# Layer norms joined with the stages behind them, and router products turned round, in a four-layer GNN and feed-forward kernel

## The reference

```python
def _layernorm(x, axis=-1, eps=1e-05):
    m = jnp.mean(x, axis=axis, keepdims=True)
    v = jnp.var(x, axis=axis, keepdims=True)
    return (x - m) / jnp.sqrt(v + eps)

x = x + _L0_gnn_ref(_layernorm(x), ...)   # edge softmax over 4 heads
x = x + _L0_ffn_ref(_layernorm(x), ...)   # the 1561 rows with the highest x @ wr + br pass a gelu MLP (256, 1024, 256)
x = x + _L1_gnn_ref(_layernorm(x), ...)   # attention with edge features, q, k, v and skip products
x = x + _L1_ffn_ref(_layernorm(x), ...)   # 32 experts, each row goes to the argmax of its logits
x = x + _L2_gnn_ref(_layernorm(x), ...)   # filter convolution, batch norm
x = x + _L2_ffn_ref(_layernorm(x), ...)   # 8 dense experts of three layers, mixed by a softmax
x = x + _L3_gnn_ref(_layernorm(x), ...)   # graph attention, batch norm
x = x + _L3_ffn_ref(_layernorm(x), ...)   # shared MLP and 4 experts, the two best gated
```

## Time and profile before

| | |
|---|---|
| median of 3 runs | 4507.1 us (4505.77 to 4510.82) |
| profiled execution | 4520.46 us, its span 4518.6 us |
| busy: PE, DVE, ACT, POOL | 3633.8, 2836.9, 1719.1, 2510.1 us |
| PE's weight loads (beside PE) | 2915.3 us |
| granted PE clock, mean | 0.861 |
| DMA | 790.42 MB, mean 175 GB/s |

### The profile page before, as it was taken

One profiled execution on the slowest core, in us unless ns is written; L12 is line 12 of the kernel. 1 busy time (PEld: TensorE's weight loads), 2 busy tenths in 40 slices (PEclk: granted clock), 3 DMA queues, 4 the chain that ended last, 5 costly groups with the idle time before them and its releaser, 6 DMA issues. The chain is left out here.

```text
span 4518.6 us, 75485 instructions
## 1 busy us (share of the span) xinstructions
PE 3633.8 (80%) x20890; PEld 2915.3 (65%) x20890; DVE 2836.9 (63%) x6154; ACT 1719.1 (38%) x3863; POOL 2510.1 (56%) x2542
## 2 busy tenths in 40 slices
PE   5997579879999999527399999479999677877288
PEld 4765457667878878425288888367777466666165
DVE  8877566458898898741488888343333345554753
ACT  3765422203333333212266666233333223333132
POOL 6885767667777777464577776200000277776300
PEclk8755779989999999758699999779999778888589
DMA  9565256279999999535488887220000167776400
GB/s 210 187 214 178 82 157 200 71 251 323 336 335 335 332 335 335 176 91 157 123 237 244 239 242 222 88 66 0 0 0 0 59 183 212 208 212 202 113 15 28
DMA packets 661732, 790.42 MB, mean 175 GB/s; under 512 B 151811, under 2 KB 584051, under 8 KB 657812
## 3 DMA queue, kind: packets, MB, share of 16 engines
q1 hardware_dynamic: 369553, 300.43, 22.6%
q0 software_dynamic: 117920, 308.04, 22.5%
q10 hardware_dynamic: 174083, 179.76, 12.9%
HBM read 516.89 MB, written 275.42 MB: 175 GB/s over the span
## 5 line engine op out<-in xcount | busy, mean ns | idle before, releaser
L2831 POOL DMA_INDIRECT fl_far<-x_table,fl_index x416 | 459.6, 1105 | 150.8 <-issue 126.5
L1596 POOL DMA_INDIRECT by_dst<-dst_row,place x416 | 434.9, 1045 | 182.8 <-issue 103.7
L2219 POOL DMA_INDIRECT a_far<-kv_table,a_index x416 | 440.3, 1058 | 140.8 <-issue 124.5
L2554 POOL DMA_INDIRECT a_far<-src_table,a_index x416 | 416.5, 1001 | 131.7 <-issue 123.1
L2868 PE MATMUL ps<-fl_w,fl_hid 128*128 128x256 f32 x1664 | 399.6, 383 | 25.7 <-ACT ps L2940 24.9
L3664 POOL DMA_INDIRECT starts<-p_out,p_at x25 | 24.7, 986 | 705.1 <-DMA starts<-p_zero 697.4
L2253 PE MATMUL ps<-a_w,a_edge_t 128*128 128x256 f32 x1664 | 397.2, 382 | 0.0
L2868 PEld LDWEIGHTS ps<-fl_w,fl_hid 128*128 128x128 f32 x1664 | 310.3, 191 | 70.7 <-issue 31.2
L2253 PEld LDWEIGHTS ps<-a_w,a_edge_t 128*128 128x128 f32 x1664 | 302.7, 192 | 33.1
L1223 ACT ACTIVATE f_hid<-ps,f_bn 128x320 f32<-128x320 f32 x320 | 197.6, 617 | 327.3 <-PE ps L1177 327.3
L1264 DVE SCALAR_TENSOR_TENSOR x_sb<-ps,f_cw,x_sb 128x256 f32 x200 | 96.8, 484 | 342.7 <-PE ps L1188 342.7
(11 more groups left out here) (583 smaller groups left out, 9314.3 us busy)
## 6 DMA issues: line engine op xcount, KB each, us to landing
partial<-a_out ACTq DMA_DIRECT2D x208, 546.0 KB
a_edge<-by_dst SPq DMA_DIRECT2D x104, 516.0 KB
partial_f<-fl_out ACTq DMA_DIRECT2D x26, 2056.0 KB
dst_row<-in_edge_attr SPq DMA_DIRECT2D x52, 1024.0 KB
xn_sb<-q_table SPq DMA_DIRECT2D x416, 128.0 KB
fl_keys<-key_rows SPq DMA_DIRECT2D x26, 1024.0 KB
a_keys<-local_rows SPq DMA_DIRECT2D x104, 128.0 KB
m_far<-kv_table SPq DMA_DIRECT2D x15, 640.0 KB, 7.2
```

Of the source, the lines that this page charges most:

```text
L1596: self.nc.gpsimd.indirect_dma_start(out=self.table, out_offset=bass.IndirectOffsetOnAxis(ap=self.place[:, n:n + 1], axis=0), in_=self.row[ ...
L2219: gathered[b % 4].count(nc.gpsimd.indirect_dma_start(out=far[:, b, u, :], out_offset=None, in_=kv_table, in_offset=bass.IndirectOffsetOnAx ...
L2554: gathered[b].count(nc.gpsimd.indirect_dma_start(out=far[:, b, u, :], out_offset=None, in_=src_table, in_offset=bass.IndirectOffsetOnAxis( ...
L2831: gathered[q * 4 + t // 4].count(nc.gpsimd.indirect_dma_start(out=far[:, q, t, :], out_offset=None, in_=table, in_offset=bass.IndirectOffs ...
```

## The change

1. `norm_stage` becomes a class `Norm` with a program part for each engine; only n4 is still a stage. The parts of n1, n2, n3, n5, n6 and n7 stand at the head of f0, p1, f1, f2, p3 and f3, so six stages end less. PE turns pair i and then follows with the products of the tiles of pair i - 2, once their copies are there. The norm has 4 (f0, f1), 6 (f2, f3) or 2 banks (p1, p3). In p1 and p3 ACT norms all tiles and copies all pairs.
2. `Router` (f1, f2, f3): 512 turned tokens (a quad of tiles) are the moving operand and the router's weights, with zeros at both sides, the stationary one, so that several quads add up in one bank, each in its own lines. ACT (in f1 also DVE) copies the lines to SBUF, PE turns them back, DVE adds the bias. The zeros are laid by POOL.
3. f0: wr, broadcast to 128 columns, is the stationary operand; each quad's product is the key row itself in all partitions. DVE adds the bias into `key_row` between its copies; PE turns 25 pieces of one line into columns for `wgt`. DVE waits for wr and br before the norm.
4. Router weights have a semaphore of their own; PE waits for the others behind the routing. f2 loads `bo` last.
5. p3's preparation (score weights, indices, zeroing of `starts` in 8 parts from a memset of 416 columns) moves to f2: SP's loads behind f2's, DVE's operations between the softmax weights and the loop. p3's copies are all DVE's, its products have 6 banks.
6. p1 has 6 banks that rotate.
7. Shares: place 27, f0 20, p1 6, f1 10 with AHEAD = 5.

```diff
+    def tensor(self, pe, follow):          # class Norm
+        BEHIND = 2
+        for i in range(self.PAIRS + BEHIND):
+            if i < self.PAIRS:
+                self.wait_normed(pe, self.tiles_of(i)[-1] + 1)
+                if i >= self.banks:
+                    self.wait_copied(pe, i - self.banks)
+                for a in self.tiles_of(i):
+                    for k in range(KD):
+                        at = (2 * k + a % 2) * P
+                        last = self.nc.tensor.transpose(self.ps[:, self.first_bank + i % self.banks, at:at + P], self.xn[:, a, k * P:(k + 1) * P], self.ident)
+                last.then_inc(self.transposed, 1)
+            if i >= BEHIND:
+                self.wait_copied(pe, i - BEHIND)
+                for a in self.tiles_of(i - BEHIND):
+                    follow(a)
...
+        if self.by_act == TILES:            # Norm.scalar, behind the last root
+            take_pairs(2, 5)
+            norm(11, 19)
+            take_pairs(5, 9)
+            norm(19, TILES)
+            take_pairs(9, self.last)
+        else:
+            take_pairs(2, self.last)
...
+    def follow(self, a):                    # class Router
+        if a % 4 != 3 and a != TILES - 1:
+            return
+        q = a // 4
+        g, i = divmod(q, self.per)
+        M, n, at = self.size(g) * self.experts, (a % 4 + 1) * P, (self.per - 1 - i) * self.experts
+        for k in range(KD):
+            last = self.nc.tensor.matmul(self.ps[0:M, self.banks[g], 0:n], self.wide[:, k, at:at + M], self.xt[:, k, q * 4 * P:q * 4 * P + n],
+                                         start=(i == 0 and k == 0), stop=(i == self.size(g) - 1 and k == KD - 1))
...
-                for a in range(TILES):                                  # f0, PE
-                    for k in range(KD):
-                        last = nc.tensor.matmul(ps[:, 7, a:a + 1], xt[:, k, a * P:(a + 1) * P], wr_sb[:, k:k + 1],
-                    nc.tensor.transpose(ps[:, a % 4, 0:P], key[:, a:a + 1].broadcast_to([P, P]), core.c("ident")).then_inc(spread, 1)
+                    q, n = a // 4, (a % 4 + 1) * P
+                    if q >= ROWS:
+                        pe.wait_ge(row_kept, q - ROWS + 1)
+                    for k in range(KD):
+                        last = nc.tensor.matmul(ps[:, 4 + q % ROWS, 0:n], wr_sb[:, k:k + 1].broadcast_to([P, P]), xt[:, k, q * 4 * P:q * 4 * P + n],
+                norm.tensor(pe, route)
+                pe.wait_ge(loaded, 64)
+                pe.wait_ge(row_kept, QUADS)
+                for a in range(TILES):
+                    last = nc.tensor.transpose(ps[:, KEYS, a:a + 1], key_row[0:1, a * P:(a + 1) * P], core.c("ident")[0:1, 0:1])
...
+                dve.wait_ge(early.router_loaded, 32)                    # f0, DVE
+                norm.vector(dve, ch, rows_ahead)
...
+                early.load(sp)                                          # f2, SP
+                project.load(sp)
...
+                project.prepare(dve, ch)                                # f2, DVE
+                dve.wait_ge(loaded, 64)
...
+                norm.vector(dve, ch)                                    # f3, DVE
+                dve.wait_ge(loaded, 240)
+                norm.wait_normed(dve, TILES)
                 for g in range(GROUPS):
                     xg = x[:, g * GROUP:(g + 1) * GROUP, :]
                     ch.add(nc.vector.tensor_tensor(xg, xg, sb3_sb[:].unsqueeze(1).broadcast_to([P, GROUP, D]), ALU.add))
...
+        norm = Norm(st, xt, banks=2, first_bank=6, by_act=TILES)        # p1 and p3
+        BANKS = 6
```

More of the change, by code:

```diff
@@ L311, in _ @@
-                root(2)
-                for a in range(7, BY_ACT):
-                    norm(a)
-                root(3)
-                take_pairs(2, LAST)
+                norm.scalar(act)
 class Windows:
@@ L383, in load, with clear_sides @@
             sp.dma_start(self.b_sb[:, i], bcast(self.biases[i])).then_inc(self.loaded, 16)
+def clear_sides(nc, wide, experts, zeroed):
+    at = Router.place(experts)
+    nc.gpsimd.memset(wide[:, :, 0:at.start], 0.0).then_inc(zeroed, 1)
+    nc.gpsimd.memset(wide[:, :, at.stop:Router.width(experts)], 0.0).then_inc(zeroed, 1)
 class L1FfnEarly(Early):
@@ L1026, in _ @@
             def _(act):
+                norm.scalar(act)
+                router.keep(act, nc.scalar.copy, 0)
                 act.wait_ge(counted, 1)
@@ L1380, in step, with route @@
                         hidden0(g, part0, 3)
-                pe.wait_ge(loaded, 272)
-                for a in range(TILES):
-                    for k in range(KD):
-                        last = nc.tensor.matmul(ps[:, 7, a * NE:(a + 1) * NE], xt[:, k, a * P:(a + 1) * P], gw_sb[:, k, :],
-                                                start=(k == 0), stop=(k == KD - 1))
-                last.then_inc(routed, 1)
+                def route(a):
+                    if a == 0:
+                        pe.wait_ge(early.router_loaded, 32)
+                        pe.wait_ge(sides_zeroed, 2)
+                    router.follow(a)
+                norm.tensor(pe, route)
+                router.turn(pe)
+                pe.wait_ge(loaded, 240)
                 step(0, 0, None, None)
@@ L3682, in _ @@
                     last.then_inc(projected, 1)
+                norm.tensor(pe, project)
             @block.scalar
             def _(act):
-                for a in range(0, TILES, 2):
-                    act.wait_ge(projected, a + 1)
-                    nc.scalar.copy(out[:, a, :], ps[:, a % BANKS, 0:SEG + HEADS]).then_inc(copied[0], 1)
+                norm.scalar(act)
             @block.vector
             def _(dve):
-                ch = Chain(dve, chain)
-                nc.vector.memset(zero[:], 0.0).then_inc(zeroed, 1)
```

586 lines of the change are left out of this document (332 added, 254 removed).

## The result

| | before | after |
|---|---|---|
| median of the runs, us | 4506.4 (4495.8 to 4510.8) | 4448.0 (4444.2 to 4453.7) |
| ratio, 95% interval | | 0.9876 (0.9859 to 0.9893) |
| span of the profiled execution, us | 4518.6 | 4451.9 |
| mean granted TensorE clock | 0.861 | 0.868 |

The change takes 58.5 us off, 1.24%; forecast were 68 (52.5 to 84.5). The profiled executions differ by 66.7. To see where, I cut the traces at the instants at which POOL clears the semaphores between two stages, and count each norm with the stage behind it.

What follows compares the result with a forecast made beforehand. Stage heads of 23 to 56 us without the stage's main work were taken as the path; gains 13 + 7 + 2.7 + 19 + 15.8 + 10.5 = 68.0 us take 4507.1 to 4439, likeliest 4427 to 4450, 8 in 10 4422 to 4470.

Steps and rivals of the forecast that it cites:

- f0: Stage f0: loop starts at +34.8 instead of +48.5 after the first statistics; gain 13 us (10 to 16).
- p3: Stage p3: first scatter at +15.1 to +15.5 instead of +31.3, POOL's pace unchanged; gain 15.8 us (14.5 to 16.5).
- f3: Stage f3, set by DVE: first weighted sum at +44.5 to +47.5 instead of +55.7; gain 10.5 us (8 to 13).
- p1, 7 forecast: Stage p1: PE ends at about +102 instead of +109.6, POOL at +105 to +106; gain 7 us.
- where POOL sets the end: Stage p1: lower bound of the gain, 4 us if POOL sets the end, against 8 where PE does.
- f2, 19 forecast: Stage f2: loop starts at about +31 instead of +49.1, p3's preparation lies in cover; gain 19 us (16 to 21).
- f1, 2.7 forecast: Stage f1: POOL stalls 7 to 8 us for a row load; sends at +67 instead of +69.9; gain 2.7 us.
- Half clock through the quads: Rival for the joined heads: clock held at 0.50, lines at about +41; gain 26 us, 4481; chance 0.08.
- f0's loop stay at half clock: Rival in f0: the loop does not regain full clock after one-column transposes; slower, up to 4639 us; chance 0.03.
- No stall in f1: Rival in f1: third item's row lands among the weights, not behind them; f1 gives 10 us, 4432; chance 0.12.
- Part is given back: Rival: two stages prove POOL- or load-bound, or DVE's late release costs f3 and f0; 25 to 50 left, about 4465; chance 0.12.

Runs made afterwards that it cites:

- e2: Changed kernel with p1's norm a stage of its own again (8 banks) and p3's preparation back in p3; 4455.7 us, ratio 0.9879 to the kernel before.
- e3: Changed kernel with p1's row loads ahead of its projection weights and f1's expert weights behind the first row load; 4438.8 us, ratio 0.9828 to the kernel before.
- e4: Changed kernel with f0's router wait moved behind the statistics, f2's root ahead of ACT's line copy, f3's shared bias earlier; 4438.9 us, ratio 0.9843.
- e6: Changed kernel with f1's expert weights behind all five row loads, f3's shared bias earlier and its first Exp ahead of hidden activations; ratio 0.9851.
- e8: Changed kernel with e4's moves, e3's p1 order, e6's Exp, f1's expert weights behind the third row load, one unread product before f2's loop; 4433.1 us, ratio 0.9820.
- e10: e8 with f1's expert weights behind the fourth row load instead of the third; 4428.3 us, ratio 0.9816 to the kernel before.
- e1: Changed kernel with the routers of f2 and f3 computed by the former narrow products inside the joined head; 4463.4 us, ratio 0.9896 to the kernel before.
- e9: e8 without the extra unread product on PE before f2's loop; 4434.7 us, ratio 0.9830 to the kernel before.

## Why the prediction was right, and where it was off

The mechanism held in f0, f1, f2, p3 and f3: the heads were the path, and shortening them moved what stands behind. In p1 the head was not the path, for POOL set the end. f0, p3 and f3 came out within 1 us of their terms, by the steps named: the weights' wait of 3.5, quads at 1.00, the first scatter at +15.5, the Exp's wait gone and DVE's order the limit. In f0 that closeness is luck, since the quads came 2.9 us late and the one-column transposes were 2.6 cheaper than priced. Two terms were mis-sized, and f1's by 2; with 55.2 for 68.0 the six stages end near the lower end of the range.

**p1, 7 forecast, 0.2 measured.** The step "POOL ... end at +105 to +106 ... Then the last stores land and the stage closes. Gain 7" failed in its last part, which had no price. PE and DVE did end 6.4 us sooner and POOL when forecast, 3.3 sooner; but now POOL ended last, with five sends issued one right behind the other, and from there to the next stage's first load 10.7 us passed (931.29 - 920.63) where it had been 7.6 (949.76 - 942.14). That eats the 3.3: 2.3 of the 3.0 are the landing, 0.65 the drain for the eight indirect DMAs more that the joined stage holds. e2 shows that the join is then worth nothing, and e3 that it is POOL's late start, behind the weights on SP's queue, which stood in the way: with the rows first the stage is 5.6 shorter. By the prediction's own numbers POOL ended last (+105 to +106, PE at +102), so its bound of 4 "where POOL sets the end" was the term that followed from them; it took 7, and 4 was still too high.

**f2, 19 forecast, 14.9 measured.** Two steps of it. The loop starts at +33.0, not +31: the logits' addition was priced at 0.4 behind the turn, but on DVE it stands behind operations that wait 2.52 us for ACT's root (e4: with the root first PE's idle is 0.99 in place of 2.00). And the half clock at the loop's start was given 1 to 1.7 less than before; it cost 1.3 more, 7.61 against 6.32. 49.1 - 33.0 = 16.1, less 1.3, is 14.8, and the stage shows 14.9. The clock's part is not the same in every execution: in e6, which leaves f2 as it is, it stays up and f2 takes 561.4, 18.7 less than before. The preparation for p3 did lie in cover (e2).

**f1, 2.7 forecast, 0.8 measured.** Stall and send time were right to half a microsecond, and the load of the sorted rows is issued 3.2 us sooner (+100.1 against +103.3). That the stage shows less is within the scatter of its loop (141.1 us before, 143.8 after). e3, e6, e8 and e10 settle the stall: it goes with the place of the weights in SP's order. Whatever stands behind the expert weights is late, be it the stage's first row load (the changed kernel), its second (e3) or its fourth (e8), or, with the weights last, the sorted rows (e6). By the Trainium skill ("DMA: Bandwidth & Descriptors", section "Queues, rings and completion order") the descriptors of one issuer's ring are, on each DMA engine, consumed in ring order; the runs agree, in that the stall followed the weights from row to row (8.17 us in the changed kernel, 9.19 in e3, 5.02 in e8).

**The rivals.** Half clock through the quads did not come: 1.00 from the second quad on in f0. e1 shows how near it was: with narrow products the same head runs at 0.50 throughout. Nor did f0's loop stay at half clock. "No stall in f1" did not come either, with 8.17 us of it. The Trainium skill ("TensorE: Matmul & The Clock Gate", "Part 4: PE-mode transpose") has the full rate not engage for transposes; here streams of eight records of transposes to four of a quad ran at 1.00. "Part is given back" came in part, through p1, by its sends.

**What stays open: when the clock falls.** In f2, behind PE's idle of 2.0 to 2.1 us, the first 16 records took 7.61, 7.58, 7.55, 5.97 and 4.57 us in five kernels whose PE program is the same there; behind 0.99 us 6.26 and 6.26; with the idle filled by products 4.57, 4.57 and 4.57, with 1.00 in all windows (first e9's window with 0.56, then e10's):

```profile
2948.00:2951.00 3.00, 3.00 (x7) 1.90 (x7) 2.81 (x6) 1.17 (x2) 0.00 (x0) 0.56 0.44 153
...
2937.00:2940.00 3.00, 2.96 (x12) 2.13 (x12) 2.25 (x7) 1.45 (x3) 0.00 (x0) 1.00 0.01 3
```

Filled it stayed up three times of three, unfilled once of seven. That speaks for the idle as the cause, but the one exception, e6, shows that an idle of 2.1 us does not always bring the fall, and f0's loop falls in two of four profiles of equal code; what decides it no run here shows. f2 is 2.1 us shorter in e8 than in e9; the medians, 4433.1 and 4434.7, can't tell such a difference.

## What to carry to other kernels

When a norm joins the stage behind, read the new head engine by engine for what now stands first in each order: here an ACT root, a bias addition and a load of weights each kept 2 to 8 us that the join had freed, and moving them brought the ratio from 0.9876 to 0.9816, some 27 us, with no arithmetic but one unread product. A load that must be early and a load that is merely large don't belong on one queue in that order; find, for each item behind it, when it is wanted. And price a stage's exit by the engine that ends last: two stages that finish at the same time on DVE can close 3 to 6 us apart when POOL still has indirect sends under way.

## What was not expected of the hardware

The exit of a stage behind POOL's indirect sends: 4.8 us until the last of five back-to-back sends had landed, and 6.00 of draining, with all engines and transfers at zero in the windows from 924 to 930. At the same place before, the landing took 2.4, the last send having waited for its tile there, and the drain 5.35. The item of eight scatters that moved into p1 costs 0.65 us of drain at its end, whether or not the sends crowd there.

Under eight-column products between 128-column transposes the clock stood at 0.50 with PE busy in 3.00 of 3.00 us (e1); under 512-column products between the same transposes it was at 1.00 from the second quad on.

The stage fl, which no kernel of this study alters, took 619.0 us in the profile of the kernel before and in the others 602.3, 602.5, 604.2, 606.8, 607.5, 608.8, 609.0, 611.2, 632.9, 633.0 and 633.4 us. A single profile's total is therefore no measure of an edit of 10 us; its stages are.
